# Column sweeps of two sweep-convolution layers: products of split fp32r parts in place of fp32 products

## The reference

```
def sweep_fwd(seq, w):
    def step(carry, row):
        new = row + jax.nn.relu(conv1d(carry, w))   # 64 -> 64 channels, 9 taps, padding 4
        return (new, new)
    _, out = jax.lax.scan(step, seq[0], seq[1:])
    return jnp.concatenate([seq[:1], out], axis=0)
...
rows = jnp.transpose(x, (2, 0, 1, 3)); rows = sweep_fwd(rows, wd); rows = sweep_bwd(rows, wu)
x = jnp.transpose(rows, (1, 2, 0, 3)); cols = jnp.transpose(x, (3, 0, 1, 2))
cols = sweep_fwd(cols, wr); cols = sweep_bwd(cols, wl)
```

## Time and profile before

| | |
|---|---|
| median of 2 runs | 5116.98 us |
| the profiled execution | 5116.51 us, span 5114.7 us |
| TensorE matmuls (PE) | 4516.3 us, 88% of the span |
| TensorE weight loads (PEld) | 3534.2 us, 69% |
| VectorE (DVE) | 1583.6 us, 31% |
| ScalarE (ACT) | 1713.7 us, 34% |
| mean granted TensorE clock | 0.758 of full |

### The profile page before, as it was taken

How to read it: one execution, slowest core, us unless ns; L and a number is a source line. 1 busy time by engine, 2 the same in 40 slices (tenths; PEclk the granted TensorE clock), 3 DMA queues, 4 the chain that set the end, 5 groups by cost and what they waited for, 6 DMA issues and landing times.

```text
span 5114.7 us, 96401 instructions
## 1 busy us (share of the span) xinstructions
PE 4516.3 (88%) x34633; PEld 3534.2 (69%) x34633; DVE 1583.6 (31%) x3154; ACT 1713.7 (34%) x5943; POOL 32.2 (1%) x73
## 2 busy tenths in 40 slices
PE   8899999987778989999998988888888888888887
PEld 2499999953336349999996346666666666666666
DVE  5755533333343675553333630000000000000000
ACT  3102344455551320123446833333333333333332
POOL 1000000000000000000000000000000000000000
PEclk9899999987786989999999965555555555555555
DMA  3100000022231530000002510000000000000000
GB/s 86 40 0 0 0 0 0 0 58 58 58 73 27 139 88 0 0 0 0 0 0 56 140 35 16 15 15 8 15 15 15 15 15 8 15 15 15 15 15 12
DMA packets 154771, 138.84 MB, mean 27 GB/s; under 512 B 87615, under 2 KB 154207, under 8 KB 154719
## 3 DMA queue, kind: packets, MB, share of 16 engines
q1 hardware_dynamic: 154718, 138.24, 11.1%
HBM read 79.18 MB, written 58.98 MB: 27 GB/s over the span
## 4 chain that ended last, share of the span: by engine, by line
PE 83%; ACT 7%; issue 5%; DVE 4%; SPq 1%; DMA 0%; ACTq 0%; DVEq 0%; POOL 0%; PEldq 0%; POOLq 0%
PE ps L716 19%; PE ps L562 18%; PE ps L637 16%; PE ps L541 15%; ACT xl L900 4%; PE ps L525 3%; PE ps L503 3%; PE ps L515 2%; ACT sums L806 2%; PE ps L581 1%; DVE img L948 1%; PE ps L630 1%; PE ps L604 1%; PE ps L594 1%; PE ps L596 1%
## 5 line engine op out<-in xcount | busy, mean ns | idle before, releaser
L716 PE MATMUL ps<-xl,vt 65*32 65x16 f32 x14400 | 1066.8, 225 | 345.1 <-ACT xl L900 345.1
L900 ACT ACTIVATE xl<-ps 64x16 f32<-64x16 f32 x3600 | 640.0, 178 | 1447.1 <-PE ps L716 1447.1
L716 PEld LDWEIGHTS ps<-xl,vt 65*32 65x32 f32 x14400 | 682.1, 141 | 617.2 <-ACT xl L900 415.3
L637 PE MATMUL ps<-img,xl 128*64 x4808 | 987.7, 293 | 4.5 <-DVE vt L1152 4.1
L562 PE MATMUL ps<-xl,taps 128*128 128x128 f32 (+2 forms) x7880 | 912.5, 279 | 4.7 <-DVE xl L1085 4.7
L562 PEld LDWEIGHTS ps<-xl,taps 128*128 128x128 f32 x7880 | 912.0, 191 | 5.5 <-issue 5.3
L541 PE MATMUL ps<-split 128*128 128x400 f32 x4140 | 790.7, 353 | 13.5 <-DVE split L1080 13.5
L541 PEld LDWEIGHTS ps<-split 128*128 128x128 f32 x4140 | 783.6, 190 | 21.0 <-issue 14.6
L637 PEld LDWEIGHTS ps<-img,xl 128*64 128x64 f32 x4808 | 695.9, 207 | 96.0 <-issue 5.6
L1160 DVE TENSOR_TENSOR xl<-xl 64x480 f32<-64x480 f32 x120 | 115.8, 965 | 1972.7 <-PEq L713 1478.5
L778 ACT ACTIVATE img<-xl 128x144 f32 x788 | 366.5, 465 | 546.9 <-DVE xl L1062 546.9
(11 more groups left out here) (131 smaller groups left out, 2005.2 us busy)
## 6 DMA issues: line engine op xcount, KB each, us to landing
ring<-in_x_dram SPq DMA_DIRECT2D x288, 100.0 KB, 2.4
x_dram<-sums SPq DMA_DIRECT2D x288, 100.0 KB, 2.2
t_dram<-sums SPq DMA_DIRECT2D x144, 100.0 KB, 2.2
ring<-t_dram SPq DMA_DIRECT2D x144, 100.0 KB, 2.4
ring<-x_dram SPq DMA_DIRECT2D x144, 100.0 KB, 2.4
xl<-x_dram SPq DMA_DIRECT2D x30, 480.0 KB, 6.3
out_dram<-xl SPq DMA_DIRECT2D x30, 480.0 KB, 4.7
img<-in_L_ffn_weight_dram SPq DMA_DIRECT2D x4, 512.0 KB
```

What stands on the lines that cost most here:

```text
L637: pe.matmul(acc[:, h * HB:(h + 1) * HB, c0:c0 + w], wsc[h], tok, start=first, stop=True, skip_group_check=True)
L716: last = pe.matmul(PS[s % 2][c * 32:(c + 1) * 32, t * B:(t + 1) * B], vt[:, c * 32:(c + 1) * 32], prev, start=False, stop=True, skip_group ...
L900: act.activation(yb[0:64, s, :, t], PS[s % 2][0:64, t * B:(t + 1) * B], ACT.Sigmoid).then_inc(step_y, 1)
```

## The change

The column sweeps get the scheme of the row sweeps. Each half step runs fifteen fp32r matmuls in place of five fp32 ones. VectorE makes the high part of the new column out of PSUM, then the column, then the low part as their difference (`column_low`). The parts lie in `split`, padded by one zero pair at each side, so the matmuls of offsets -1, 0 and 1 are 144 columns wide and those of -2 and 2 are 128. The accumulators alternate between two pairs of PSUM banks (`column_bank`), for which TensorE's loop is unrolled by two. Ahead of the column stage the padded parts are blanked (four casts of 128x160), the first columns are split, and the column taps are split: the high part on ScalarE after the relayout, the low part on VectorE, after which TensorE may begin.

```diff
+        def column_part(h, part):
+            return split_line(h, part).rearrange("p b j -> p (b j)")[:, 0:HB * (HP + 2)].rearrange("p (b j) -> p b j", b=HB)
...
+        def column_bank(u, k, h):
+            return PS[2 * ((u + k) % 2) + h][:, 0:HB * HP].rearrange("p (b j) -> p b j", b=HB)
...
         def pe_columns(pe, l, k):
-            with pe.Fori(0, STEPS[k]) as s:
+            def step(su, x):
+                s, u = su
                 for h in range(2):
-                    acc = PS[h][:, 0:HB * HP].rearrange("p (b j) -> p b j", b=HB)
-                    pe.wait_ge(state[l][h], s + LINES0[k])
+                    acc = column_bank(u, k, h)
+
+                    def products(tap_part, line_part):
+                        for d in OFFS:
+                            t0 = ((k - 2) * NO + d + 2) * 128
+                            j0, j1 = (0, HP) if abs(d) < 2 else (max(0, -d), min(HP, HP - d))
+                            ins = pe.matmul(acc[:, :, j0:j1], taps_part[tap_part][:, t0:t0 + 128],
+                                            column_part(h, line_part)[:, :, 1 + j0 + d:1 + j1 + d],
+                                            start=(tap_part == line_part == 0 and d == OFFS[0]),
+                                            stop=(line_part == 1 and d == OFFS[-1]))
+                        return ins
+
+                    pe.wait_ge(hi[l][h], s + LINES0[k])
                     own(pe)
-                    for n, d in enumerate(OFFS):
-                        lo, hi = max(0, -d), min(HP, HP - d)
-                        last = pe.matmul(acc[:, :, lo:hi], taps[:, (k * NO + d + 2) * 128:(k * NO + d + 3) * 128],
-                                         column[h][:, :, lo + d:hi + d], start=(n == 0), stop=(n == NO - 1))
-                    last.then_inc(conv[l][h], 1)
+                    products(0, 0)
+                    products(1, 0)
+                    pe.wait_ge(lo[l][h], s + LINES0[k])
+                    own(pe)
+                    products(0, 1).then_inc(conv[l][h], 1)
+
+            each_column(pe, k, step)
...
             pe_rows(pe, l, 1)
+            pe.wait_ge(taps_lo[l], 2)
             pe_columns(pe, l, 2)
...
+        def split_column_taps(act, l):
+            for h in range(2):
+                act.wait_ge(conv[l][h], STEPS0[2])
+            act.activation(taps_part[0], taps[:, 2 * NO * 128:4 * NO * 128], ACT.Copy).then_inc(taps_hi[l], 1)
...
             act_relayout(act, l)
+            split_column_taps(act, l)
             act_columns(act, l, 2)
...
+        def column_low(dve, l, h, after):
+            dve.wait_ge(hi[l][h], after)
+            dve.wait_ge(state[l][h], after)
+            own(dve)
+            dve.tensor_tensor(column_part(h, 1)[:, :, 1:1 + HP], column[h], column_part(h, 0)[:, :, 1:1 + HP], ALU.subtract
+                              ).then_inc(lo[l][h], 1)
+
         def dve_columns(dve, l, k):
...
+                    dve.scalar_tensor_tensor(out=column_part(h, 0)[:, :, 1:1 + HP], in0=acc, scalar=0.0, in1=column_at(l, h, x),
+                                             op0=ALU.max, op1=ALU.add).then_inc(hi[l][h], 1)
                     dve.scalar_tensor_tensor(out=column[h], in0=acc, scalar=0.0, in1=column_at(l, h, x), op0=ALU.max, op1=ALU.add
                                              ).then_inc(state[l][h], 1)
+                    column_low(dve, l, h, s + (LINES0[k] + 1))
...
             for h in range(2):
+                dve.wait_ge(lo[l][h], LINES0[2] - 1)
+                for part in range(2):
+                    dve.tensor_copy(column_part(h, part), pick[:, 0:1].broadcast_to([128, HB, HP + 2])).then_inc(blank, 1)
+            for h in range(2):
                 dve.wait_ge(relaid[l][h], 3 * HP)
                 dve.tensor_copy(column[h], column_at(l, h, 0)).then_inc(state[l][h], 1)
                 dve.sem_inc(put_back[l][h], 1)
+                dve.wait_ge(blank, l * 4 + 4)
+                dve.tensor_copy(column_part(h, 0)[:, :, 1:1 + HP], column_at(l, h, 0)).then_inc(hi[l][h], 1)
+                column_low(dve, l, h, LINES0[2])
+            dve.wait_ge(taps_hi[l], 2)
+            dve.tensor_tensor(taps_part[1], taps[:, 2 * NO * 128:4 * NO * 128], taps_part[0], ALU.subtract).then_inc(taps_lo[l], 1)
```

More of the change, by code:

```diff
@@ L175, in metaformer @@
         relaid = [[sem(f"relaid{l}_{h}") for h in range(2)] for l in range(2)]
+        blank = sem("blank")
         put_back = [[sem(f"put_back{l}_{h}") for h in range(2)] for l in range(2)]
@@ L231, in each_column @@
                 for u in range(2):
-                    step(q * 2 + u, eng.snap(column_x(k, q, u)))
+                    step((q * 2 + u, u), eng.snap(column_x(k, q, u)))
             if STEPS[k] % 2:
-                step(STEPS[k] - 1, column_x(k, STEPS[k] // 2, 0))
+                step((STEPS[k] - 1, 0), column_x(k, STEPS[k] // 2, 0))
+        def column_bank(u, k, h):
+            return PS[2 * ((u + k) % 2) + h][:, 0:HB * HP].rearrange("p (b j) -> p b j", b=HB)
         def each_step(eng, k, step):
@@ L773, in act_columns, with step @@
         def act_columns(act, l, k):
-            def step(s, x):
+            def step(su, x):
+                s, u = su
                 for h in range(2):
```

## The result

The changed kernel takes 6732.98 us (two runs, 6729.63 and 6736.33) against 5116.98: 1.3156 times the time, 95% interval 1.3132 to 1.318. The prediction said 6,730 us and slower.

A forecast was written before the change was run, and what follows sets the result against it. TensorE's column stream was taken as the bound, the new matmuls bound by weight loads at half clock: 5,116.5 minus 912.5, plus 788 x 15 x 0.213 = 2,518, plus 2 x 4, gives 6,730 us; range 6,150 to 6,880.

The forecast's parts named there:

- Products: Column stages: fifteen fp32r matmuls per half step, bound by weight loads, 3.20 us at half clock or 1.68 at full.
- lower end: Column products at half clock: loads only 0.167 us apart, 2.5 us per half step, giving 6,182 us.
- The rival product of the Trainium skill: Column products: if fp32r gets the quick weight load, streaming bounds them at 0.98 us per half step.
- Clock: Column stages: both begin at half clock after a longer TensorE wait and stay there, PEclk 0.50 from end to end.
- the first rival: Column stages: full clock, columns start slow but recover or never fall; 5,540 us, chance 0.12.
- VectorE: Column half step: three operations, about 1.28 us, up to 1.35 with the turnaround, hidden beside the other half's products.
- Start: Ahead of the column stage: blanking and splitting columns and taps delay TensorE 4 us more per layer, idle about 6.4 us.
- The other side: Column product stream: faster outcome if loads are hidden, three passes replacing four, 0.86 us instead of 1.156 per half step.
- The fourth rival: Column product stream: loads under 0.06 us and VectorE below 1.13 us make it faster, best 4,890 us; chance 0.02.
- Sum: Whole kernel: 5,116.5 us minus 912.5, plus 2,518 for the new products, plus 2 x 4 for the starts: 6,730 us.

The follow-up runs named there:

- the filled wait: Changed kernel with ten extra fp32 matmuls of 400 columns ahead of the columns in both layers: 5541.69 us; with twenty: 5546.66 us.
- a burst between the sweeps: Changed kernel with twenty extra fp32 matmuls between the right and left sweeps of each layer, the wait ahead of the columns left: 6178.34 us.
- the wide ones: Changed kernel whose ten products on the line's high part also stream the low part, 288 or 256 columns, extra columns thrown away: 5791.69 us.
- half-load kernel: Changed kernel with 64 instead of 128 weight columns in every column product, half of the outputs not computed: 5221.54 us.

## Why the prediction was right, step by step

- **Products.** Forecast 15 x 0.213 at half clock, measured 15 x 0.2134; at full clock, where the filled wait put them, 0.112 against 0.1117. The step from L663's fp32 loads to fp32r loads held: three ways of changing the load or the number of matmuls gave what load-bound matmuls give. (The text calls a load 256 cycles at either level; by its own 0.112 us it is 268 at full clock, which costs nothing here.) The lower end taken from L515's pair (0.167 us) was wrong: it is a distance between two loads, not the pace of a long run of them.
- **The rival product of the Trainium skill.** The rule in the Trainium skill, "TensorE: Matmul & The Clock Gate", section on fast weight load, that quick loads engage for 128 weights of a type other than FP32, did not show for fp32r: 0.1117 us per matmul at full clock with 128 weight columns, the pace of L663's fp32 loads, and 0.0735 with 64.
- **Clock.** Forecast half clock from end to end in both layers, seen so. The argument had two steps, and the runs show that both were needed. The first is the start: a longer wait (forecast idle 6.4 us, measured 6.24), in which the clock falls. With the wait filled, or a burst between the sweeps, the same stream runs at 1.00, and the first rival's 5,540 us is the kernel with the filled wait (5,542). The second is the stream: after the same wait the fp32 products, the wide ones and those with half the load also began at 0.50, and were at 1.00 within 3 to 6 us; the changed kernel's never came back. This second step was taken by likeness ("no row shows that one"), and the likeness to L663 was not close: L663's stream began at 1.00 and was down at 0.50 2 us later, while the new one keeps 1.00 for 659.5 us. That it fell on the right side was in part luck, and 0.12 was little for the first rival: its reason, that a clock once up stays up, holds for this stream (for L663's it doesn't), and 7 us of work ahead of each stage are all that separates the two times.
- **VectorE.** Forecast 1.28 us, up to 1.35 with the turnaround, hidden beside 3.2 us. Measured 0.33 + 0.54 + 0.31 = 1.18, and 1.277 as a pace where it bounds, in the half-load kernel. The last operation was the mis-sized one (0.41 forecast by the PSUM operation, 0.31 measured for one that reads SBUF alone). It cost nothing here.
- **Start.** 4 us per layer forecast, 3.9 measured.
- **The other side.** The fourth rival needed a load under 0.06 us and VectorE below 1.13 us. With loads of 64 columns and the low part left out, the products' own pace of 0.0735 us was left, more than the 0.0573 in that rival's price: 5,067 us, far from its 4,890.
- **Sum.** 5116.5 - 912.5 + 2,522 + 8 = 6,734 against 6732.98 measured.

## What to carry to other kernels

Count weight loads as well as passes. Here an fp32 product was two records with a load each, and its three fp32r passes are three: ten loads per half step became fifteen. Where the rows' 400-column matmuls of the same scheme run at 0.19 us each, the narrow ones pay for a load of 0.112. From these times I estimate the width at which both cost the same at full clock: three loads take 3 x 0.1117 = 0.335 us at any width up to there, and two fp32 records take 2 x 0.1156 = 0.231 us at 134.4 columns. If the fp32 ones grow with the width, they reach 0.335 us at about 195 columns. No run was made near it. Then look at what TensorE did just before a long uniform stage: here seven microseconds of useless matmuls per layer were worth 1,190 us, because the same stream ran on at whichever clock it began with. Filling pays where the queue would be empty anyway, as ahead of a stage; inside the dependent loop of the recurrence the filler delayed the very matmul that was waited for. Not tested: taps split earlier, so that the wait ahead of the columns stays at 2.35 us. The kernel before lost the clock after such a wait in one of its two layers, so it might not be enough. And with the clock kept, the change is still 8% slower than the kernel before.

## What the runs showed that I had not expected

- This stream, bound by its weight loads, keeps either clock for a whole stage: 0.50 for 1,261 us, and 1.00 for 659 us, with identical instructions. Other streams after the same wait come back from 0.50, and L663's falls from 1.00: three behaviours under an engine that is busy 100% of the time or nearly so.
- An fp32r matmul of 137.6 columns with a load of 64 takes 0.0735 us at full clock, more than its columns (0.057) or half of a 128-column load (0.056). What the rest is stays open.
- In the recurrence at 1.00 the step with its filler took 0.685 us in the mean, longer than the 0.576 us of the unfilled step at 0.50.
